# A language-model tower on one Trainium2 core: five row buffers for sorted experts, an earlier unit, a later expert

## The reference

```python
xm = _ln(x, ln2_g, ln2_b)
logits = xm @ gate_w.T + gate_b
topv, topi = jax.lax.top_k(logits, TOPK)
gates = jax.nn.softmax(topv, axis=-1)
onehot = jax.nn.one_hot(topi, NEXP, dtype=x.dtype)
comb = jnp.einsum('bnk,bnke->bne', gates, onehot)
moe_out = jnp.zeros_like(x)
for e in range(NEXP):
    he = jax.nn.gelu(xm @ exp_w1[e] + exp_b1[e], approximate=False)
    oe = he @ exp_w2[e] + exp_b2[e]
    moe_out = moe_out + comb[..., e:e + 1] * oe
return x + moe_out
```

## Time and profile before

| | |
|---|---|
| median of 3 runs | 966.93 us (966.31 to 968.48) |
| time of the profiled execution | 968.75 us |
| its span in the trace | 967.0 us |
| busy: PE, PEld, DVE, ACT, POOL | 800.1, 720.1, 548.2, 473.9, 332.8 us |
| mean granted clock of PE | 0.913 of full |
| mixer's end up to chunk 11 | until about 662.6 us |
| gating, scatters, chunks 12 to 23 | 662.6 to 735.7 us |
| groups and output | 735.7 to 967.0 us |

### The profile page before, as it was taken

The page is one execution under the profiler, slowest core; times in us unless marked ns, Lnnn a source line. Parts: engine busy times, 40 slices in busy tenths (PEclk is TensorE's granted clock), DMA queues, the critical chain, the costliest instruction groups (busy, mean ns, idle before and its releaser), DMA issues.

```text
span 967.0 us, 17260 instructions
## 1 busy us (share of the span) xinstructions
PE 800.1 (83%) x6072; PEld 720.1 (74%) x6072; DVE 548.2 (57%) x1453; ACT 473.9 (49%) x1328; POOL 332.8 (34%) x529
## 2 busy tenths in 40 slices
PE   0489999999999999847789999999794768676683
PEld 0379999999999999836678888877673667565673
DVE  5764545454645453548779776577982544344442
ACT  2254444545444444306758898744553443443431
POOL 6461011111102020213464555537564242342423
PEclk9899999999999999978979999999797887887877
DMA  8333232424142332339200100021122121221213
GB/s 251 87 79 99 43 103 54 102 56 99 55 86 66 75 75 66 75 123 231 71 1 2 59 18 1 2 90 58 62 68 72 22 42 26 38 34 30 43 26 73
DMA packets 59268, 64.31 MB, mean 67 GB/s; under 512 B 8656, under 2 KB 53840, under 8 KB 59152
## 3 DMA queue, kind: packets, MB, share of 16 engines
q1 hardware_dynamic: 50896, 53.60, 22.6%
q0 software_dynamic: 6416, 7.54, 4.5%
q10 hardware_dynamic: 1872, 2.08, 0.7%
HBM read 36.25 MB, written 28.12 MB: 67 GB/s over the span
## 4 chain that ended last, share of the span: by engine, by line
PE 18%; issue 16%; DVE 8%; POOL 6%; DMA 3%; ACT 2%; POOLq 1%; SPq 0%; ACTq 0%; DVEq 0%
POOL home_rows L1288 2%; POOL mix_w_dense L1278 2%; PE mix_ring L1405 2%; PE mix_ring L1354 2%; PE mix_ring L1417 2%; PE mix_ring L1376 2%; PE mix_scores L1343 1%; PE mix_ring L1316 1%; DMA mix_stage<-in_w 1%; PE mix_ring L1520 1%; PE mix_ring L1367 1%; PE mix_ring L1463 1%; DVE mix_w_all L1728 1%; ACT mix_probs L1582 1%; PE mix_ring L1382 1%
## 5 line engine op out<-in xcount | busy, mean ns | idle before, releaser
L454 POOL TENSOR_SCALAR attn_probs<-attn_probs,attn_inverse 128x128 f32<-128x128 f32 x128 | 48.2, 376 | 288.4 <-DVE attn_inverse L744 280.6
L1211 POOL TENSOR_SCALAR mix_probs<-mix_probs,mix_inverse 128x128 f32<-128x128 f32 x192 | 73.9, 406 | 65.5 <-DVE mix_inverse L1768 65.5
L1288 POOL DMA_INDIRECT home_rows<-mix_total,mix_group_rows x30 | 47.1, 1570 | 135.4 <-DVE mix_total L1926 128.3
L613 ACT ACTIVATE attn_probs<-ps_scores,attn_neg_max 128x128 f32<-128x128 f32 x128 | 45.4, 366 | 77.9 <-DVE attn_neg_max L740 77.9
L1903 DVE TENSOR_TENSOR mix_hid_lo<-mix_gelu,mix_hid_hi 128x512 fp32r<-128x512 f32 x45 | 51.2, 1155 | 50.8 <-ACT mix_hid_hi L1674 50.7
L1582 ACT ACTIVATE mix_probs<-mix_scores,mix_neg_max 128x128 f32<-128x128 f32 x192 | 67.8, 391 | 2.0 <-DVE mix_neg_max L1760 1.9
L1540 PE MATMUL mix_scores<-mix_w_all,mix_hid_hi 128*128 x180 | 68.2, 428 | 0.3 <-DVE mix_hid_lo L1903 0.3
L1520 PE MATMUL mix_ring<-mix_xt_hi,mix_w_dense 128*128 128x256 f32 x270 | 65.7, 317 | 2.7 <-DVE mix_xt_lo L1895 2.7
L1670 ACT ACTIVATE mix_gelu<-mix_ring,mix_group_b 128x256 f32<-128x256 f32 x90 | 37.8, 471 | 61.7 <-PE mix_ring L1520 44.6
L1380 PE MATMUL mix_ring<-ident,mix_group_rows 128*128 128x128 f32 x30 | 13.1, 438 | 61.1 <-DMA mix_group_rows<-sorted_rows 61.1
L627 ACT ACTIVATE attn_mixed_rows<-ps_mixed 128x512 f32<-128x512 f32 x32 | 19.3, 604 | 84.6 <-PE ps_pairs L544 84.6
(11 more groups left out here) (357 smaller groups left out, 2714.0 us busy)
## 6 DMA issues: line engine op xcount, KB each, us to landing
v_rows<-attn_v_flat SPq DMA_DIRECT2D x16, 768.0 KB, 3.3
attn_v_rows<-v_rows SPq DMA_DIRECT2D x128, 96.0 KB, 3.8
sorted_rows<-mix_xt_full SPq DMA_DIRECT2D x28, 197.0 KB, 8.2
mix_group_rows<-sorted_rows SPq DMA_DIRECT2D x15, 197.0 KB, 2.5
mix_stage<-in_w SPq DMA_DIRECT2D x5, 576.0 KB, 5.7
mix_stage<-in_w SPq DMA_DIRECT2D x10, 192.0 KB, 3.1
mix_stage<-in_w SPq DMA_DIRECT2D x5, 384.0 KB, 4.3
attn_stage_main<-in_w_qkv SPq DMA_DIRECT2D x2, 768.0 KB, 7.4
```

What stands on the lines that cost most here:

```text
L454: last = nc.gpsimd.tensor_scalar(probs[:, n, j, :], probs[:, n, j, :], inverse[:, n, j:j + 1], float(D) ** -0.5, ALU.mult, ALU.mult)
L613: last = nc.scalar.activation(probs[:, n, j, :], ps_scores[:, n % 2, j, :], ACT.Exp, bias=neg_max[:, n, j:j + 1], accum_out=sums[:, n, j:j ...
L1211: last = nc.gpsimd.tensor_scalar(turn, turn, inverse[:, i, s:s + 1], 1.0, ALU.mult, ALU.mult)
L1288: nc.gpsimd.indirect_dma_start(dram["home"], bass.IndirectOffsetOnAxis(ap=group_rows[:, g % 3, b, ROW - 1:ROW].bitcast(I32), axis=0), tota ...
```

## The change

It has three parts.

1. `DEEP = 5`: the row buffers `group_rows` go from three to five, the bias buffers `group_b1` and `group_b2` from two to three. SP's waits become: the rows of g when g-5 is home; the biases of g when group g-3 has read its first-layer biases and begun its sums.
2. Unit 1's whole gating and its scatter move into the hand-written lists, between the mixer's last heads and dense steps. For this `logits`, `chosen` and `exps` are doubled, and unit 1's halves lie in `hid_hi` and `hid_lo`. Unit 1's EN1.6 comes earlier, unit 2's EN goes there too, and on POOL the additions of the residual (B) of units 1 and 2 and the scatter come before the bias products (WEIGH). Units 2 and 3 are gated within the third expert (chunks 12 to 17), their scatters hang behind chunks 16 and 17.
3. The first unit's last expert, chunks 18 to 23 (`EARLY = 18`), moves behind the groups. `place(i)` numbers the chunks in the new order. Its first two first layers stand among the last second layers of group 14; its first second layer waits until the sums of all 15 groups have left `ps_out`. The sums of groups now lie in `bias_sum` instead of `total`, so they no longer wait until unit 0's rows are stored. These are stored tile by tile at the very end, behind the copy of the home rows.

Besides, some semaphores are merged, and the first loop of a group's sums (L1923) waits after each operation on VectorE's own counter.

```diff
+    DEEP = 5
...
-        group_b1 = sb("group_b1", [P, 2, HC])
+        group_b1 = sb("group_b1", [P, 3, HC])
...
-        group_rows = sb("group_rows", [P, 3, GROUP_TILES, ROW])
-        group_b2 = sb("group_b2", [P, 2, D])
-        group_x = (xt_hi[0], xt_lo[0])
+        group_rows = sb("group_rows", [P, DEEP, GROUP_TILES, ROW])
+        group_b2 = sb("group_b2", [P, 3, D])
+        group_x = (xt_hi[2], xt_lo[2])
...
+        EARLY = 3 * HC
+        put(FIRST, ("EX", (2, 0)), ("EX", (2, 1)), ("EN", (3, 0)), ("EN", (3, 1)))
+        put(FIRST + 1, *(("EN", (3, part)) for part in range(2, NORM_PARTS - 1)), ("EG", 2))
+        put(FIRST + 2, ("EN", (3, NORM_PARTS - 1)), ("B", 3), ("EB", 2), ("RANK", 2))
+        put(FIRST + 3, ("EX", (3, 0)), ("EX", (3, 1)), ("EXP", 2), ("CNT", 2))
+        put(FIRST + 4, ("GATES", 2), ("SLOT", 2), ("SCATTER", 2), ("EG", 3))
+        put(FIRST + 5, ("EB", 3), ("RANK", 3), ("EXP", 3), ("CNT", 3), ("GATES", 3), ("SLOT", 3), ("TABLE", 0), ("SCATTER", 3))
...
+        place = lambda i: i if i < EARLY else len(blocks) + i
+        both = [("L1", i) for i in range(FIRST - LAG, EARLY)] + [("G1", i) for i in range(len(blocks))] + [("L1", i) for i in range(EARLY, len(chunks))]
...
+                if g >= DEEP:
+                    sp.wait_ge(came_home, 16 * GROUP_TILES * (g - DEEP + 1))
...
                 if g >= 3:
-                    sp.wait_ge(came_home, 16 * GROUP_TILES * (g - 2))
...
+                    sp.wait_ge(chunk_read, EARLY + BLOCKS * (g - 2))
+                    sp.wait_ge(biased_group, g - 2)
...
-                if g == 0:
-                    sp.wait_ge(expert_free, NEXP * UNIT)
-                    sp.dma_start(dram["out"][0:UT, :].rearrange("(b p) d -> p b d", p=P), total[:, :, :]).then_inc(first_stored, 16)
             sp.wait_ge(came_home, 16 * GROUP_TILES * SORTS)
             sp.dma_start(dram["out"][UT:TOKENS, :], dram["home"][0:SORTED * UT, :]).then_inc(out_stored, 16)
-            sp.wait_ge(first_stored, 16)
-            sp.wait_ge(out_stored, 16)
+            for b in range(UNIT):
+                sp.wait_ge(expert_free, (NEXP - 1) * UNIT + b + 1)
+                sp.dma_start(dram["out"][b * P:(b + 1) * P, :], total[:, b, :]).then_inc(out_stored, 16)
+            sp.wait_ge(out_stored, 16 * (1 + UNIT))
...
+                if i == EARLY:
+                    pe.wait_ge(group_free, GROUP_TILES * SORTS)
...
-                if g < 2:
-                    dve.wait_ge(first_stored, 16)
-                else:
+                if g >= 2:
                     dve.wait_ge(came_home, 16 * GROUP_TILES * (g - 1))
-                dve.wait_ge(group_weights[g % 2], 32 * (g // 2 + 1))
-                mine = lambda b: total[:, g % 2 * GROUP_TILES + b, :]
+                dve.wait_ge(group_weights[g % 3], 32 * (g // 3 + 1))
+                mine = lambda b: bias_sum[:, g % 2 * GROUP_TILES + b, :]
```

More of the change, by code:

```diff
@@ L997, in mixer_and_feed_forward, with second_of @@
         order = []
[L998 to L1001, removed]
         blocks = [(g, k) for g in range(SORTS) for k in range(BLOCKS)]
-        def second_block(i):
+        place = lambda i: i if i < EARLY else len(blocks) + i
+        both = [("L1", i) for i in range(FIRST - LAG, EARLY)] + [("G1", i) for i in range(len(blocks))] + [("L1", i) for i in range(EARLY, len(chunks))]
+        def second_of(step, i):
+            if step == "L1":
+                second(i)
+                return
             g, k = blocks[i]
@@ L1011, in second_block @@
                 order.append(("GA", g))
-        order.append(("GW1", 0))
-        order.append(("GX", 0))
-        for i, (g, k) in enumerate(blocks):
-            order.append(("G1", i))
-            if k == 0 and g + 1 < SORTS:
-                order.append(("GW1", g + 1))
-            if k == 1 and g + 1 < SORTS:
-                order.append(("GX", g + 1))
-            if i >= LAG:
-                second_block(i - LAG)
-        for i in range(len(blocks) - LAG, len(blocks)):
-            second_block(i)
+        for n, (step, i) in enumerate(both):
+            if n < LAG:
+                continue
+            if (step, i) == ("G1", 0):
+                second_of(*both[n - LAG])
+                second_of(*both[n - LAG + 1])
+                order.append(("GW1", 0))
+                order.append(("GX", 0))
+            order.append((step, i))
+            if step == "G1":
+                g, k = blocks[i]
+                if g + 1 < SORTS and k < 2:
+                    order.append((("GW1", "GX")[k], g + 1))
+            if not (step == "G1" and i < LAG):
+                second_of(*both[n - LAG])
+            if step == "L1":
+                order.extend(after.get(i, ()))
+        for step, i in both[-LAG:]:
+            second_of(step, i)
         slot_of, slots = {}, 0
@@ L1441, in logits_of @@
                 for n, (g, x, part) in enumerate(passes):
-                    last = nc.tensor.matmul(ring[0:NEXP, bank("EG", u), :], g[:, :], x[min(u, 1)][:, part, :], start=n == 0, stop=n == 4)
+                    last = nc.tensor.matmul(ring[0:NEXP, bank("EG", u), :], g[:, :], x[min(u, 2)][:, part, :], start=n == 0, stop=n == 4)
                 last.then_inc(g_filled, 1)
@@ L1622, in split_x @@
                 act.wait_ge(xt_full_ready, n)
[L1623 removed]
+                nc.scalar.activation(xt_hi[min(u, 2)][:, part, :], xt_full[:, part, :], ACT.Copy).then_inc(xt_hi_ready, 1)
             def gate_halves(_):
@@ L1666, in group1 @@
                 if k == 0:
-                    act.wait_ge(group_weights[g % 2], 32 * (g // 2 + 1))
+                    act.wait_ge(group_weights[g % 3], 32 * (g // 3 + 1))
                 for c in range(2):
                     part = slice(c * GT, (c + 1) * GT)
-                    last = nc.scalar.activation(gelu[:, n % 2, part], ring[:, bank("G1", i), part], ACT.Gelu, bias=group_b1[:, g % 2, 2 * k + c:2 * k + c + 1])
+                    last = nc.scalar.activation(gelu[:, n % 2, part], ring[:, bank("G1", i), part], ACT.Gelu, bias=group_b1[:, g % 3, 2 * k + c:2 * k + c + 1])
                 last.then_inc(chunk_read, 1)
@@ L1934, in in_two @@
                         else:
-                            dve.wait_ge(hid_used, (out + 1) * HC)
+                            dve.wait_ge(hid_used, place((out + 1) * HC - 1) + 1)
                         first(b + 1).then_inc(expert_added, 1)
```

218 lines of the change are left out of this document (84 added, 134 removed), and 4 rows, old and new, of the table ORDERS.

## The result

The changed kernel takes 915.84 us in the median of four runs (913.1 to 917.01), the kernel before 966.76 (four runs); the ratio is 0.9466 (0.9442 to 0.949). Forecast were 891 us and a range of 872 to 919: the time lies in the range, near its upper end, and the gain is 51 us where 76 were expected. The profiled execution took 917.01 us, its span is 915.3 us, and its mean clock 0.943.

What follows compares the result with a forecast made beforehand. Three row buffers were taken to bound the groups, a gating and scatter chain the stretch before. Parts 1 to 3, -73.6 - 4.7 + 2.2 = -76, took 968.75 us to 892.6, 891 as median; range 872 to 919.

Steps and rivals of the forecast that it cites:

- the first turn: Start of the groups' rows on PE, after gating and scatters: expected at 731 us, a change of -4.7 (-13 to +4).
- a round: One group to the next in the groups' stretch: 8.9 us instead of 14.56, bounds 8.4 and 10.2, 13 times.
- the tail: From group 14's first layer to the kernel's end: 31 us instead of 28.8, +2.2 (-2 to +5).
- the ring: Groups before the change: home transfer, load, turn, split and layers follow each other through three row buffers, 14.56 us a round.
- 2.98 - 0.69 (split's end to sum's end): Term of the 8.9 us round: VectorE's time from the end of a group's split to the sum POOL waits for.
- about 0.5: Term of the 8.9 us round: the held split finishing on VectorE after POOL's cast, estimated between 0 and 1.17 us.
- cast holds all: Rival for the groups: every low half meeting POOL's cast waits for it, and PE too; round 10.2, 908 us, chance .13.
- So the mixer's end grows by about 7: Mixer's end with unit 1's gating and scatter added: about 7 us longer, bounds +2 and +12.
- some 9.5 us: Mixer's end on VectorE: delay from some 30 instructions put before the two later parts of an expert's weight split.
- PE alone: Rival for the groups: nothing on VectorE is held where the loop closes; round 8.4 us, time 885 us, chance .15.
- Slower: Rival: PE's clock stays at its lower level through groups and tail; rounds 15.0 us, time 980 us, chance .04.
- Rows or clock in part: Rival for the groups: half the row wait stays, or clock stays 0.79; rounds 10.5 to 11.3, 917 us, chance .10.

## Why the prediction was right, and where it was off

The profiled execution was put at 892.6 us and took 917.01, 24.4 more. By its own steps: the first turn was put at 731 and came at 746.0 (15.0); a round was put at 8.9 and took 9.56 (13 x 0.66 = 8.6); the tail was put at 31 and took 31.6; 0.2 is from first turn to group 1.

**Part 1, mechanism right, one term too small.** Five row buffers open the ring, as the run with part 1 alone shows; a loop of VectorE, POOL and the cast is next, as the forecast had it. The step that failed is the term "2.98 - 0.69 (split's end to sum's end)", which lets the split itself be held and be over with the cast. The term "about 0.5" behind the cast was right in size (0.48). What the cast holds is not the split but a low half ahead of it, and the split follows in full: 3.22 us from the split's start to the end of the sums instead of 2.29. With it the loop is 9.71, between the forecast's 8.9 and the 10.2 of the rival "cast holds all", whose mechanism (a low half is held, the split and PE behind it) is nearer the truth. The mean of 9.56 has the first rounds in it, which are shorter. Section 8 (Key points) of the Trainium skill's GPSIMD Engine Reference names this contention for VectorE instructions with two SBUF inputs; the low half's 3.71 us beside a cast, and 0.69 without one, agree.

**Part 2, the mixer's end, wrong.** The step that failed is "So the mixer's end grows by about 7", with its bounds of +2 and +12: it grew by 22.6, and the first turn came after 740, the prediction's own sign that part 2 is wrong. The next unit's rows are turned behind it, in PE's timeline of the kernel before at

```profile
663.57 0.60 PE L1429 MATMUL mix_ring<-ident,norm_zn 128*128 128x128 f32 x4
```

and of the change at

```profile
686.18 0.60 PE L1399 MATMUL mix_ring<-ident,mix_later_rows 128*128 128x128 f32 x4
```

The path that the prediction named is in the chain of waits of the change too:

```profile
654.22 1.37 DVE mix_w_all L1704
...
657.39 5.29 DMA mix_stage<-in_w
```

From the last part of the weight split (L1704, L1728 before) to the turning of the next unit's rows were 33.3 us before, and 32.0 now. So the growth arose ahead of it: this part came 24.0 us later than in the earlier trace rows, where "some 9.5 us" were forecast for 30 instructions of VectorE ahead of the two later parts. That term counted their busy time and left out what they wait for, and it let the first part come as before; but this one was already 18.4 us late (638.12 after 619.71). PE stood 4.2 us for unit 1's split, which stood behind a softmax on ScalarE, and 4.1 for the counts, and the clock fell behind both waits, where before it was 1.00. From 600 to 686 us PE was idle for 11.8 us (2.0 in the earlier trace rows) and busy for 74.2 (60.6), unit 1's added work and the slower clock together; these two were not told apart. VectorE in turn stood 6.5 us for PE between the parts of its weight split. Part of the wait for the counts is the contention of part 1 again: the first four operations of a rank took 3.16 us from 633.12 on, beside POOL's copies (632.46 to 636.18), and 0.91 from 636.75 on, behind them. The lists put otherwise bring 10 us back; which of these waits carries how much stays open.

**The rest of part 2, right.** From that turn to the groups' first turn I had put some 60 us and the trace has 59.8; the scatters of units 2 and 3 follow one another within 10.7 us (10.3 forecast), and 6.0 us after the last issue comes the turn (5.86). But this saving of 12 us is less than the mixer's end lost.

**Part 3, right.** Tail 31.6 (31); the last dense first layer starts 22.5 us after group 14's first layer, below the 25 of its sign. That PE's chunks take nothing off ahead of the groups is what the run with them there shows.

**The rivals.** "PE alone" failed because of the cast. Rounds of 8.3 came only when it left POOL. "Slower" needed the low clock in the groups; it was 0.96 there, 0.50 for the first 10 us behind PE's wait of 14.9 us, and 1.00 from 761 to 881 us:

```profile
800.00:840.00 40.00, 35.33 (x268) 31.31 (x266) 31.64 (x49) 24.79 (x51) 22.58 (x14) 1.00 0.36 57
```

The rule on psum-queue depth-cycling in the Trainium skill's TensorE: Matmul & The Clock Gate would have the clock swing with micro-idles between groups of matmuls; with a wait of 1.2 us in each of these rounds this trace does not show that. "Rows or clock in part" didn't occur; with two bias buffers it did in part (10.2 us a round).

## What to carry to other kernels

When a ring of buffers is opened, write down the next loop operation by operation, and ask which instruction of the other engine meets the long one: behind a held instruction everything in its queue starts late in full. A step that is moved into a stretch where PE is the bound must be judged by the waits its written place makes on every engine, not by its busy time. And try the parts of a change apart: here one part gave 66 us, one took 14, one nothing.

## What was not expected of the hardware

A VectorE subtraction of two SBUF operands that had begun 0.45 us before a POOL cast did not end beside it, but 0.56 us after it. Three casts in a row held it as long as one (3.91 us against 3.71). POOL's home additions, 1.5 to 2.4 us each, held nothing. The same cast takes 1.36 us on VectorE and 2.70 on POOL.
